# Reordered queues: results, loads and stores inside the attention rounds, the hand-over from graph to attention, and the values of the second direction in the prologue

## What is computed

```
self = [x, q] @ W_self.T + b_self                       # graph block
for d in (0, 1):                                        # two directions of the label tensor
    aff = (self @ Wq[d].T) . (self[:, :20] @ Wk[d].T)   # 16 heads of 32, 20 keys
    w = softmax(where(count > 0, aff, NEG) + label_bias)
    out += (w @ self[:, :20]) @ Wout[d]                 # per head
x1 = x + relu(self + out)
h = gamma * layernorm(x1) + beta                        # gamma, beta: two products of the condition
q, k, v = h @ Wqkv.T                                    # attention block, 16 heads of 32, 512 keys
h1 = (softmax(q k) / sqrt(512) @ v) @ Wp.T + bp + x1
y = (gamma * layernorm(h1) + beta) + h1
```

## Time and profile before

| | us |
|---|---|
| median of 3 timed runs (lowest, highest) | 1351.17 (1349.26, 1354.97) |
| the profiled execution | 1355.45 |
| its span, first to last instruction | 1353.6 |
| mean granted TensorE clock | 0.966 |
| PE busy / DVE / ACT / POOL | 1248.8 / 891.5 / 615.2 / 882.3 |

### The profile page before, as it was taken

How to read it: one execution, slowest core, us unless ns; L and a number is a source line. 1 busy time by engine, 2 the same in 40 slices (tenths; PEclk the granted TensorE clock), 3 DMA queues, 4 the chain that set the end, 5 groups by cost and what they waited for, 6 DMA issues and landing times.

```text
span 1353.6 us, 20343 instructions
## 1 busy us (share of the span) xinstructions
PE 1248.8 (92%) x6100; PEld 831.7 (61%) x6100; DVE 891.5 (66%) x1448; ACT 615.2 (45%) x1076; POOL 882.3 (65%) x565
## 2 busy tenths in 40 slices
PE   7879899999999788899999999999999999999983
PEld 4347677777777666466656666666565566566551
DVE  3445578778778754756766776776675776676745
ACT  1322252445244434454454464464464455455452
POOL 1114467676776734765795796795796696696733
PEclk9979899999999888899999999999999999999987
DMA  9663254445444653433543442542442542542410
GB/s 340 253 224 110 63 191 172 157 158 222 159 155 146 202 192 89 126 86 72 149 110 71 135 124 67 142 123 65 139 127 56 144 116 69 145 116 69 115 47 32
DMA packets 104454, 178.60 MB, mean 132 GB/s; under 512 B 38832, under 2 KB 48368, under 8 KB 99104
## 3 DMA queue, kind: packets, MB, share of 16 engines
q1 hardware_dynamic: 92816, 145.22, 35.3%
q10 hardware_dynamic: 11536, 32.14, 7.9%
HBM read 81.04 MB, written 45.38 MB: 93 GB/s over the span
## 4 chain that ended last, share of the span: by engine, by line
PE 29%; DVE 12%; POOL 9%; issue 6%; DMA 3%; ACT 3%; SPq 1%; ACTq 0%; DVEq 0%; POOLq 0%
PE a_bank L1808 6%; PE a_bank L1759 6%; DVE rden L1653 5%; POOL acc L1361 4%; PE a_bank L1772 4%; PE a_bank L106 4%; DVE keep L1635 4%; PE a_bank L107 4%; PE a_bank L108 4%; PE a_bank L1819 2%; DMA out_y<-h 1%; ACT pt L1526 1%; POOL acc L1356 1%; DMA h<-h_rows 1%; DVE rden L1661 1%
## 5 line engine op out<-in xcount | busy, mean ns | idle before, releaser
L1635 DVE TENSOR_REDUCE keep<-a_bank 128x1 f32<-128x512 f32 x496 | 331.5, 674 | 256.5 <-PE a_bank L1772 254.1
L1526 ACT ACTIVATE pt<-a_bank 128x512 f32<-128x512 f32 x512 | 300.5, 597 | 376.5 <-PE a_bank L1759 322.9
L1361 POOL TENSOR_TENSOR acc<-acc,pt 128x1024 f32<-128x1024 f32 x120 | 286.5, 2387 | 32.4 <-ACT pt L1526 25.2
L1759 PE MATMUL a_bank<-sq_stack,sk_stack 98*128 98x512 f32 x512 | 221.7, 433 | 19.6 <-ACT pt L1526 7.5
L1772 PE MATMUL a_bank<-sk_stack,sq_stack 96*128 96x512 f32 x496 | 209.4, 422 | 4.5 <-DVE keep L1635 4.4
L1356 POOL TENSOR_TENSOR acc<-pt 128x1024 f32<-128x1024 f32 x60 | 143.6, 2393 | 77.4 <-PE a_bank L1819 65.4
L1759 PEld LDWEIGHTS a_bank<-sq_stack,sk_stack 98*128 98x128 f32 x512 | 98.0, 191 | 115.5 <-issue 71.7
L1065 PE MATMUL g_bank<-m,sf 128*128 128x320 f32 x512 | 147.5, 432 | 0.8 <-issue 0.8
L1653 DVE RECIPROCAL rden<-a_bank 128x128 f32<-128x128 f32 x128 | 120.6, 944 | 17.9 <-PE a_bank L1802 17.9
L1772 PEld LDWEIGHTS a_bank<-sk_stack,sq_stack 96*128 96x128 f32 x496 | 95.9, 193 | 48.6 <-DVE keep L1635 33.0
L1808 PE MATMUL a_bank<-pt,v 128*32 128x512 f32 x1024 | 124.7, 605 | 0.0
(11 more groups left out here) (200 smaller groups left out, 2496.0 us busy)
## 6 DMA issues: line engine op xcount, KB each, us to landing
sq_stack<-qh SPq DMA_DIRECT2D x256, 64.0 KB, 2.0
sk_stack<-kh SPq DMA_DIRECT2D x256, 64.0 KB, 2.1
m<-m_rows SPq DMA_DIRECT2D x8, 1280.0 KB, 6.7
xraw<-in_x_t SPq DMA_DIRECT2D x8, 1024.0 KB, 8.8
xn<-in_x SPq DMA_DIRECT2D x8, 1024.0 KB, 5.2
h_rows<-xn ACTq DMA_DIRECT2D x8, 1024.0 KB, 4.8
t_rows<-houth SPq DMA_DIRECT2D x8, 1024.0 KB, 3.9
t_rows<-houtl SPq DMA_DIRECT2D x8, 1024.0 KB, 6.5
```

Source lines behind the costliest of these rows:

```text
L1361: nc.gpsimd.tensor_tensor(acc[:, two, :], acc[:, two, :], pt[:, step + 1, two, :], ALU.add).then_inc(s["sum_done"], 1)
L1526: nc.scalar.activation(pt[:, i, 2 * half + k, :], bank[:, k, :], ACT.Exp).then_inc(s["exp_done"], 1)
L1635: nc.vector.reduce_max(mx[:, half, k, n:n + 1], bank[:, 2 + e % 2, :], AX).then_inc(s["emax_done"], 1)
L1759: nc.tensor.matmul(bank[:, k, :], sk[c % 2][0:3 * DH + 2, j, i * P:(i + 1) * P], sq[c % 2][0:3 * DH + 2, j, :], start=True, stop=True).the ...
```

## The change

Prologue: `values_in` of direction 1 moves to units 16 to 23 (its `values_out` behind units 22 and 25), `gamma_beta` to units 24 to 31; the loads of `wout[1]` and `wq[1]` go ahead of those of `wg` and `wb`; the stores of the second direction's values and of the two products are issued among the last `m_rows` stores.

Graph: DVE scales the bias `bcol3` after the steps and not before them; in the last step the four `add_bp` follow all of the softmax; SP issues `stacks(1, 1)` (the copy that was the first of the attention block) before the shift row; the last two stores `t_rows` become DMAs of the attention block, behind the load of `wp_raw`.

Attention: `result` of tiles 1, 2 and 3 moves to the start of round 2, the start of round 3 and the end of round 3 (before: start of round 2 behind `rsqrt`, inside round 2, start of round 3). `normalise`, `load_h`, `load_t`, `store_y` and `load_rows` move with it, `project` of the queries goes from slot 4 to 3, `lo_part` from slots 5 and 9 to 3 and 10, two reciprocals one slot later, `quotients` to slot 9, `output_hi` to slot 10.

```diff
@@ prologue, sync @@
-            store_v(1)
-            sp.wait_ge(s["gb_step"], 6)
-            sp.dma_start(d["gb_rows"][:, 0, :], gs8[:, :]).then_inc(s["st_gb"], 16)
-            sp.dma_start(d["gb_rows"][:, 1, :], bs8[:, :]).then_inc(s["st_gb"], 16)
+                if i == 2 * FC - 3:
+                    store_v(1)
+                if i == 2 * FC - 2:
+                    sp.wait_ge(s["gb_step"], 6)
+                    sp.dma_start(d["gb_rows"][:, 0, :], gs8[:, :]).then_inc(s["st_gb"], 16)
+                    sp.dma_start(d["gb_rows"][:, 1, :], bs8[:, :]).then_inc(s["st_gb"], 16)
@@ prologue, vector @@
-                if 6 * FC - 1 <= n < 7 * FC - 1:
-                    gamma_beta(n - 6 * FC + 1)
-                if n in (7 * FC - 1, 8 * FC - 1):
-                    values_out(n // FC - 4)
+                if n in (5 * FC + 2, 6 * FC + 1):
+                    values_out(n // FC - 3 if n < 6 * FC else 3)
+                if 8 * FC - 1 <= n < 9 * FC - 1:
+                    gamma_beta(n - 8 * FC + 1)
@@ prologue, tensor @@
-                elif n < 4 * FC:
+                elif n < 6 * FC:
                     values_in(n // FC - 2, n % FC)
-                elif n < 6 * FC:
-                    gamma_beta(n // FC - 4, n % FC)
                 elif n < 8 * FC:
-                    values_in(n // FC - 4, n % FC)
+                    gamma_beta(n // FC - 6, n % FC)
@@ graph, sync @@
             stacks(1, 0)
+            stacks(1, 1)
...
-            store_t(B - 1, 4 * B)
+            sp.wait_ge(s["hl_done"], 4 * B)
@@ graph, gpsimd @@
-                        if has_former:
+                        if has_former and not last:
                             add_bp(b - 1, i - 2)
+                if last:
+                    for i in range(NT):
+                        add_bp(b - 1, i)
@@ attention, sync @@
-                    if c < 3 or more:
+                    if (c < 3 or more) and not start(b, c):
                         stacks(*ahead(b, c, 1), 1)
                     shift_lo(b, c, 1)
                     if c == 2 and later:
                         store_y(b - 1, 1)
                     if c == 3 and later:
-                        store_y(b - 1, 3)
-                    if c == 3:
-                        load_rows(b)
+                        store_y(b - 1, 2)
+                    if c == 0 and not first(b) and not (isinstance(b, int) and b == 1):
+                        store_y(b - 2, 3)
+                    if c == 0 and later:
+                        load_rows(b - 1)
                     if c < 2 or more:
-                        stacks(*ahead(b, c, 2), 0)
+                        stacks(*ahead(b, c, 2), 0, (0,))
+                    if c == 1 and later:
+                        store_y(b - 1, 0)
+                    if c < 2 or more:
+                        stacks(*ahead(b, c, 2), 0, (1,))
                     if c < 3 or more:
                         shift_lo(*ahead(b, c, 1), 0)
-                    if c == 1 and later:
-                        store_y(b - 1, 0)
-                    if c == 2 and later:
-                        store_y(b - 1, 2)
@@ attention, gpsimd @@
+                    if later and c > 1:
+                        result(b - 1, c - 1)
                     if later and c in (1, 2):
                         rsqrt(b - 1, 2 * c - 2)
-                    if later and c in (2, 3):
-                        result(b - 1, 2 * c - 3)
                     if not final(b, c):
                         key_sum(b, c, 0, 0)
-                    if later and c in (1, 2):
-                        result(b - 1, 2 * c - 2)
+                    if later and c == 1:
+                        result(b - 1, 0)
...
+                    if later and c == 3:
+                        result(b - 1, 3)
@@ attention, scalar @@
-                        if slot == 2 and c in (2, 3) and later:
-                            normalise(b - 1, 2 * c - 3)
+                        if slot == 2 and c == 2 and later:
+                            normalise(b - 1, 1)
+                        if slot == 4 and c == 3 and later:
+                            normalise(b - 1, 3)
...
-                        if slot == 4 and (c < 2 or more):
+                        if slot == 3 and (c < 2 or more):
                             project(*ahead(b, c, 2), 0)
-                        if slot == 5 and c in (1, 2) and later:
+                        if slot == 4 + c and c in (1, 2) and later:
                             normalise(b - 1, 2 * c - 2)
...
-                            if slot == 15 and c == 1:
+                            if slot == 13 and c == 1:
                                 load_h(b - 1, 2)
...
-                        if slot == 1 and c == 3 and more:
-                            load_h(b, 0)
-                        if slot == 10 and c == 3 and more:
-                            load_h(b, 1)
+                        if slot == 6 and c == 0 and later:
+                            load_h(b - 1, 0)
+                        if slot == 8 and c == 0 and later:
+                            load_h(b - 1, 1)
...
-                        if slot == 11 and c == 1 and more:
+                        if slot == 14 and c == 1 and more:
                             load_t(b + 1, (1,))
-                        if slot == 9:
+                        if slot == 10:
                             if c == 0 and later:
                                 output_hi(b - 1, 3)
@@ attention, vector @@
-                        if slot == 5 and (c < 2 or more):
-                            lo_part(*ahead(b, c, 2), 0)
                         if slot == 3:
                             shift_lo(b, c, 1)
-                        if 4 <= slot < 8 and former:
-                            reciprocals(*former, slot - 4)
-                        if slot == 8 and former:
+                            if c < 2 or more:
+                                lo_part(*ahead(b, c, 2), 0)
+                        if slot in (4, 5, 7, 8) and former:
+                            reciprocals(*former, slot - 4 - slot // 6)
+                        if slot == 9 and former:
                             quotients(*former)
...
-                        if slot == 9 and (c < 2 or more):
+                        if slot == 10 and (c < 2 or more):
                             lo_part(*ahead(b, c, 2), 1)
```

More of the change, by code:

```diff
@@ L469, in graph @@
         assert nc.sbuf_base == at["out"]
-        houth, houtl = sb("houth", [P, FC, N], F32R), sb("houtl", [P, FC, N], F32R)
+        houth, houtl = t["houth"], t["houtl"] = sb("houth", [P, FC, N], F32R), sb("houtl", [P, FC, N], F32R)
         assert nc.sbuf_base == at["acc"]
@@ L658, in label_products, with softmax @@
                     [P, NT * 2 * NK, L]), ALU.mult).then_inc(s["adjw_done"], 1)
-            def softmax(b, has_former):
+            def softmax(b, has_former, last=False):
                 for i in range(NT + 2):
@@ L709, in step @@
                     lo_rows(b - 2)
-                softmax(b, True)
+                softmax(b, True, last)
             pool.wait_ge(s["set_up"], 3)
@@ L1006, in step @@
                     labels(b + 1)
-            dve.wait_ge(la["ld_c"], 16)
-            nc.vector.tensor_scalar(bcol3[:, 2, :], bcol3[:, 2, :], float(D) ** -0.5, None, ALU.mult).then_inc(la["bv_done"], 1)
             nonzero_rows(0)
@@ L1016, in _ @@
             steps(dve, step)
+            dve.wait_ge(la["ld_c"], 16)
+            nc.vector.tensor_scalar(bcol3[:, 2, :], bcol3[:, 2, :], float(D) ** -0.5, None, ALU.mult).then_inc(la["bv_done"], 1)
             lo_part(0, 0)
@@ L1276, in _, with stacks @@
         def _(sp):
-            def stacks(b, c, half):
+            def stacks(b, c, half, which=(0, 1)):
                 G, par = 4 * b + c, c % 2
@@ L1282, in stacks @@
                     sp.wait_ge(s["et_ready"], SLOTS * (G - 2) + 8 * half + 8)
-                for ready, src, dst, at, done in (
-                        (s["qh_done"], qh, sq, (0, 2 * DH), stq), (s["ql_done"], ql, sq, (DH,), stq),
-                        (s["kh_done"], kh, sk, (0, DH), stk), (s["kl_done"], kl, sk, (2 * DH,), stk)):
+                for n, ready, src, dst, at, done in (
+                        (0, s["qh_done"], qh, sq, (0, 2 * DH), stq), (0, s["ql_done"], ql, sq, (DH,), stq),
+                        (1, s["kh_done"], kh, sk, (0, DH), stk), (1, s["kl_done"], kl, sk, (2 * DH,), stk)):
+                    if n not in which:
+                        continue
                     sp.wait_ge(ready, need)
@@ L1319, in batch @@
                     if c == 3 and later:
-                        store_y(b - 1, 3)
-                    if c == 3:
-                        load_rows(b)
-                    if c < 2 or more:
-                        stacks(*ahead(b, c, 2), 0)
+                        store_y(b - 1, 2)
[3 more added lines that the diff above has]
+                        load_rows(b - 1)
+                    if c < 2 or more:
```

(10 more changed lines are left out.)

4 lines of the change are left out of this document (2 added, 2 removed).

## The result

The changed kernel takes 1332.53 us in the median (1327.03 to 1338.32), the one before 1351.76 beside it: ratio 0.9848, 95% interval 0.9805 to 0.9890. It is faster, clear of the noise, but by 1.5%: 19 us where 49 were forecast. The time lies 4.5 us above the top of the range for 8 in 10 (1292 to 1328).

A forecast was written before the change was run, and what follows sets the result against it. Attention rounds were taken as PE-bound work stretched by three queues. Terms -22.0 - 16.2 - 9.2 - 2.6 + 1.5 - 0.5 = -49.0 us, which on the median of 1351.17 gives 1302; range for 8 in 10: 1292 to 1328.

The forecast's parts named there:

- prologue: Before the graph: value stores leave the end, but product steps slow the last units; -0.5 us, bounds -3.3 and +1.5.
- graph: End of the graph: ACT's first eviction 2.8 us later behind four additions in a row; net +1.5 us, bounds -2 and +2.5.
- batch 0: Attention's first batch: earlier copies of stacks(1, 1) save 7.1 us including the lower clock, rounds 1 to 3 2.1; 9.2 us.
- batches 1 to 6: Steady attention rounds: 22.0 us from DVE's slots and 16.2 us from POOL, stores and loads.
- batch 7 and tail: Last attention batch: rounds 0 and 1 give 1.5, round 2 2.0, round 3 loses 0.9; 2.6 us; tail untouched.
- The failed step: Steady batches, round 2, slot 2: load_t's second half lands at 27.0, needed at 26.7; 0.3 us lost a batch.
- rival 1: Load_t's late half: loads of 8.4 us in round 1 cost 3 us a batch, 18 in all; 1318 us, chance 0.18.
- DVE's 22.0: Steady rounds of batches 1 to 6: DVE's lateness no longer stops PE, 0.92 of 0.95 us on 24 rounds; bounds 0 and 22.8.
- the 19.2 of POOL, stores and loads: Batches 1 to 6, rounds 1 to 3: waits on POOL, stores and loads go; 19.2 less 3 for new tightness, 16.2 us.
- Rival 2: Steady rounds: DVE's lateness only moves, slots 8 to 12 stretch as before; 26 us less gain, 1328 us, chance 0.13.
- Rival 3: Round 1: SP waits for result 0 ahead of the key copies and POOL's lateness stops PE; slower, 1358 us, chance 0.03.
- the 10 us and 6.7 us: Graph's end, by the exclusion rule alone: additions waiting out subtractions take 10 us, the eviction comes 6.7 us later; not booked.

The follow-up runs named there:

- h15: Changed kernel with load_h of tile 2 at slot 15 of round 1 instead of slot 13: 1312.9 us, ratio 0.9727 to the kernel before.
- h15 with `add_bp` inside: h15 with the four add_bp of the graph's last step between the products e * rc again: 1308.1 us, ratio 0.9690 to the kernel before.
- the version with quarters: h15 with the second half of load_t in two quarters, each with its own semaphore: 1305.8 us, ratio 0.9669 to the kernel before.
- the load at slot 13: Changed kernel with the second half of load_t at slot 13 of round 1, ahead of load_h, instead of slot 14: 1334.4 us, ratio 0.9866.
- the load at slot 11: Changed kernel with only the second half of load_t back at slot 11 of round 1, from 14: 1324.3 us, ratio 0.9803.

## Why the prediction missed, step by step

Against the profiled span, booked and measured:

| term | booked | measured |
|---|---|---|
| prologue | -0.5 | -4.8 |
| graph | +1.5 | +1.55 (410.90 to 412.45) |
| batch 0 | -9.2 | -8.7 |
| batches 1 to 6 | -38.2 | -3.3 |
| batch 7 and tail | -2.6 | -5.0 |

**The failed step** is the landing of the second half of `load_t`: "is issued about 20.6 to 21.3 us into round 1", takes "median 5.8", "so it lands at 27.0". I booked 0.3 us a batch, with 3 as the bound and as rival 1; it cost 2.0 once and 6.2 to 6.6 five times, 34 us in all. Three things were wrong in it.

- The issue, by 1.7 us. I placed it by its slot and did not read what stands ahead of it on ACT: `load_h`, moved to slot 13, waits for the store of tile 0, which the prediction puts at 15.3 (measured 15.54) and gives no landing time; it takes 6.1. Shown by h15: one line, 20 us. (That line also takes 0.25 MB out of the load's way, and the low half takes 5.3 to 6.6 us in place of 6.2 to 8.7; the run does not part the two.)
- The duration, by 1.8 us. The median of the earlier trace rows mixes first and second halves, and high parts with low ones, which are issued later and land last. The one that matters took 5.8 to 8.3 before, and 6.2 to 8.7 here.
- The clock. Of the 34 us, 21.1 are PE's idle time and most of the other 12.9 the lower clock behind it. A 3 us bound has no room for that, though I had booked just such a term, 2.9 us, for the first round.

Rival 1 was thus right in kind, and its price, 18 us, was half of the true one. With the pauses taken off, batches 1 to 6 of the changed kernel are 580.0, where the forecast less its own 3 us for tightness gives 617.3 - 41.2 = 576.1. Of the 3.9 between, some 0.9 is the pause where the loop turns back (3.2 us here, beside the earlier trace rows), whose cause stays open, 0.7 a late end of round 1 in batch 2, and the rest rounds 0 and 3 of 24.0 to 24.2 us where 23.9 were booked.

**Near in sum, wrong in its parts:** DVE's 22.0 and the 19.2 of POOL, stores and loads. DVE's lateness costs 0.7 in rounds 0 and 3 and 0.5 in rounds 1 and 2, not 0.92 in all: 14.5. (The 0.95 that it was taken from is a slip too: 24.82 less the 23.8 of the sum is 1.0; against the measured floor of 23.9 it is 0.9.) The other term then is 617.3 - 580.0 - 14.5 = 22.8, so that two errors of opposite sign hid part of each other, which is luck. Nor can the two be had apart: DVE's slots give 5 us alone and 12 to 18 where the landings are in time. Rival 2 did not come: no stretch in slots 8 to 12. Rival 3 neither: the key copies go at 16.1 us into round 1, behind the store.

**Batch 0** came out at 8.7 of 9.2, and part of that is luck: h15 and h15 with `add_bp` inside have the same code there and take 100.8 and 101.2, not 98.2, with a third round of 28.0 and 28.1 us where this trace has 25.2.

**The prologue** was sized wrongly, by 4.3 in this pair of traces and by 2.7 in the mean of all: the five product steps did not slow the units (last `m_rows` issued at 80.96, where the kernel before has 81.82). **The graph's end** was right: first eviction 2.9 later (2.8 booked), net 1.55 (1.5). Timeline of POOL and DVE there, changed kernel:

```profile
451.74 6.28 POOL L690 TENSOR_TENSOR xn<-xn,bp 128x512 f32<-128x512 f32 x4
451.82 6.75 DVE L979 TENSOR_TENSOR wvl<-v,wvh 128x512 fp32r<-128x512 f32 x4
```

One subtraction of the same kind with nothing on POOL, from DVE's timeline of the changed kernel:

```profile
420.61 0.68 DVE L979 TENSOR_TENSOR wqkl<-v,wqkh 128x512 fp32r<-128x512 f32 x1
```

The prediction's price for this place rests on a misread row. Its 1.22 for a subtraction is the mean of four of which three ran beside POOL's arithmetic; alone one takes 0.68. One after the other, four additions of 1.28 and four subtractions of 0.68 are 7.8 us, not 10. The trace has all eight done in 6.8: each subtraction begins inside an addition, takes 1.75 and ends 0.56 after the addition does, and each addition behind a subtraction takes 1.71. So they go nearly one after the other, 1 us short of it over all eight. That is close to the whole exclusion that the Trainium skill ("SBUF — State Buffer", section "SBUF: two separate sides") states, and the 10 us and 6.7 us that the prediction works out by that rule are too high because of the 1.22. The 2.8 that was booked came from the rows and holds.

**Batch 7:** round 3 and the tail lost 0.9 as booked; round 2 gained 4.6, not 2.0, since its pauses of 1.87 us in slot 3 and 1.56 in slot 8 are gone, and with the second the lower clock behind it (slots of 2.3, 2.1 and 1.9 us).

## What to carry to other kernels

A transfer that is moved is issued only when its engine gets there. Read every wait ahead of it in that queue, those moved in the same change above all, and do not trust the releaser named on the next compute row when a DMA issue stands between. Price its landing by the same DMA in the same traffic, not by a median over a line. Where PE would pause, add the lower clock to the price: here it was some 12 us beside 21 of idle time. Edits that shorten rounds do not add up with transfers that keep their length: the same move of `load_t` was worth -7 us and +8 us in two versions. And ask of a cure whom it makes late next: `load_h` at slot 15 freed ACT and made DVE's residual wait in the version with quarters.

## What the runs showed of the hardware

A copy of 4 KB landed 2.8 us after its issue with the load of 1 MB behind it, and 6.6 with the load 1.7 us ahead; the DMA share in the gap was full (1.06, 245 GB/s). The row and the key copies go by SP's queue, the load by ACT's. The Trainium skill ("DMA: Bandwidth & Descriptors", section "Queues, rings and completion order") has each DMA engine serve its queues in turn; that fits, and no run here isolates it.

The granted clock was at its lower level after PE idled 3.6 us (0.50 over the next 3.4 us). After shorter pauses both levels are found, for the same pause too: with the load at slot 13, PE idled 2.44 us ahead of round 2 in batch 1 and went on at 0.50 (slots of 2.27, 2.20 and 1.97 us), and idled 2.44 us at the same place in batch 6 and went on at 1.00 (1.25, 1.20, 1.26). With the load at slot 11 the clock was lower after 1.75 us in batch 5 and full after 2.64 us in batch 2. In the attention rounds of the fourteen traces every longer pause, of 2.7 to 4.8 us, was followed by the lower level. The same pause can so cost an execution 2.7 us (slot 13, batch 1 against batch 6) or nothing.
